# Cross-attention and mixture-of-experts kernel: unrolled two-expert tiles taken two at a time by TensorE

## The chip, the cores and the metric

One core of a Trainium2 chip runs the whole kernel in one launch. The metric is the device time of one execution in microseconds; the median of three runs is taken. The core's engines are TensorE (matrix products and transposes, results in PSUM), VectorE, ScalarE, GpSimd (named POOL in the profile, here mostly the issuer of gathers) and SyncE, which issues DMAs. Each works through its own list of instructions in order and waits on semaphores that the others raise.

## The reference

After a layer norm and a cross-attention, whose softmax is added to x, the second half is a mixture of experts over 1024 rows of 256 numbers. 64 experts have 64 hidden features each, and every row goes to 4 of them:

```python
_, topk_idx = jax.lax.top_k(logits + router_bias, K)          # K = 4
...
g = jnp.einsum('nd,edf->enf', flat, Wg)
u = jnp.einsum('nd,edf->enf', flat, Wu)
h = jax.nn.silu(g) * u
hw = h * combine.T[:, :, None]
out = jnp.einsum('enf,efd->nd', hw, Wd)
for i in range(Sg.shape[0]):                                   # 2 shared experts
    sh = jax.nn.silu(flat @ Sg[i]) * (flat @ Su[i])
    out = out + sh @ Sd[i]
```

The kernel computes only the chosen experts' products: rows are gathered into tiles by expert, and the results are gathered back and summed with their weights. All is float32.

## The kernel before

Attention, norms, routing and the lists of rows take the first 63 us. Then come tiles of 128 rows. The first `NP` = 32 tiles are unrolled, and each serves two experts: lanes 0 to 63 hold rows of expert 2q, lanes 64 to 127 rows of expert 2q+1. After them come tiles for the rows that did not fit, one expert each, whose experts are known only at run time; two turns of `U` = 4 such tiles are unrolled and the rest is a hardware loop. At the end the shared experts' products are computed and the results are gathered back.

One tile passes through these operations:

- GpSimd gathers 128 rows into `xg`, four buffers (L362; semaphore `got`). The gather of tile t waits for the transposes of tile t-4.
- TensorE transposes the two halves of the tile into bank `pb0` or `pb1` (L1014, semaphore `xT_ps`). It first waits for `xT_sb`, the copy of tile q-2 that empties the bank.
- VectorE copies the bank to `xgT`, two buffers (L805, semaphore `xT_sb`).
- TensorE makes the first product, gate and up together, into `pb2` or `pb3` (L1047, `gu_ps`). For a two-expert tile it is four matmuls of 64 output lanes each, half of the array's columns ("128*64" in the profile). One-expert tiles use two matmuls on the whole array (L1051).
- ScalarE applies silu to the gate half (L494, `silu_ok`).
- VectorE multiplies it with the up half into `hh2`, two instructions, one for each expert's lanes (L819, `h_ok`).
- TensorE transposes `hh2` into bank `pb7` (L1070, `hT_ps`); ScalarE copies it to `hT` (L503, `hT_sb`).
- TensorE makes the second product into `pb4` or `pb5` (L1083, `y_ps`), ScalarE copies it to `ysb` (L513, `y_sb`), and SyncE stores it.

The order is written out by hand. `over_tiles` calls each engine's function `step` for s = 0, 1, 2, ... and `which(lag)` gives it tile s - lag. In step s TensorE takes the input transposes of tile s, the first product of tile s-1, the `hh2` transpose of tile s-2 and the second product of tile s-3. VectorE takes the copy of tile s and `hh2` of tile s-1; ScalarE the silu of s-1, `hT` of s-2 and `ysb` of s-3.

VectorE carries other work in the same list, behind `hh2` of its step: one-hots for the token lists (`one_hot`, L680 and L682, s = 1, 3, 5, 7), a reduction (L835, s = 9), the token list (`tokens`, s = 11), the tiles' experts (`tile_experts`, L745 on, s = 12), two choices in each of s = 13 to 28 (`pick_choice`, L768) and the weights of the choices (`weights_of_choices`, L775 on, s = 29). ScalarE's `value` (L476) and TensorE's `list_tokens` (L984) belong to the token lists too.

Of the kernel before, what the change touches and what calls it, by code (L numbers as in the profile page):

```python
# [33 lines left out]
DC = D // P  # L34
HB = P // 2
NP = E // 2
MAXOV = 64
# [11 lines left out]
U = 4  # L49
# [10 lines left out]
def build_xattn_moe(nc, x, proj, amask, kmask, router, task, b2, rbias, shared, wgu, wd, out):  # L60
# [3 lines left out]
    with ExitStack() as ctx:  # L64
# [341 lines left out]
        def _(act):  # L406
# [75 lines left out]
            for n in range(1, EARLY):  # L482
                unit(n)

            def step(which, k, first, s):

                tile = which(1)
                if tile:
                    pair, q, m, r = tile
                    n = m % 2  # L490
                    act.wait_ge(gu_ps, q + 1 if pair else q + (NP + 1))
                    if not pair or q >= 2:
                        act.wait_ge(h_ok, q - 1 if pair else q + (NP - 1))
                    a.activation(sg[:, n, :], pb[2 + n][:, 0:F], ACT.Silu).then_inc(silu_ok, 1)  # L494
                tile = which(2)
                if tile:
                    pair, q, m, r = tile
                    n = m % 2
                    at = q if pair else q + NP
                    act.wait_ge(hT_ps, at + 1)  # L500
                    if not pair or q >= 2:
                        act.wait_ge(y_ps, at - 1)
                    a.activation(hT[:, n, :], pb[7][:, 0:P], ACT.Identity).then_inc(hT_sb, 1)  # L503
                tile = which(3)
                if tile:
                    pair, q, m, r = tile
                    n = m % YB
                    act.wait_ge(y_ps, q + 1 if pair else q + (NP + 1))
                    if pair and q >= YB:
                        act.wait_ge(y_out[n], 16 * (q // YB))  # L510
                    elif not pair:
                        act.wait_ge(y_out[n], r * (16 // YB) + 16 * NP // YB)
                    a.activation(ysb[:, n, :], pb[4 + m % 2][:, 0:D], ACT.Identity).then_inc(y_sb, 1)  # L513
                if s in (2, 4, 6, 8):
                    value((s - 2) // 2, MAXOV, NR)

            over_tiles(act, step, 4, lambda: (turn_count(act), last_turn_end(act)))
            for n in range(EARLY, len(units)):
# [365 lines left out]
        def _(pe):  # L884
# [115 lines left out]

            pe.wait_ge(unit_sb, 2)

            def step(which, k, first, s):

                tile = which(0)
                if tile:
                    pair, q, m, r = tile
                    n = m % 2
                    at = q if pair else q + NP
                    pe.wait_ge(got[m], 16 * (q // XB + 1) if pair else r * (16 // XB) + (NP // XB + 1) * 16)  # L1010
                    if not pair or q >= 2:
                        pe.wait_ge(xT_sb, at - 1)
                    for h in range(DC):
                        ins = t.transpose(pb[n][:, h * P:(h + 1) * P], xg[:, m, h::DC], ident[:, :])  # L1014
                    ins.then_inc(xT_ps, 1)

                if s == NP - 2:

                    pe.wait_ge(at_ok, 2)
                    for reg, e in zip(next_gu, load_at(0)):  # L1020
                        pe.reg_mov(reg, e)
                if s is None or s >= NP:

                    if k == 0:
                        gu_of[:] = [pe.snap(reg, min_val=0, max_val=E - 1) for reg in next_gu]
                    if k < D_LAG - GU_LAG:
                        if s is None or s >= NP + U:
                            d_of[k] = pe.snap(last_gu[k], min_val=0, max_val=E - 1) // 2
                    else:
                        d_of[k] = gu_of[k - (D_LAG - GU_LAG)] // 2  # L1030
                tile = which(GU_LAG)
                if tile:
                    pair, q, m, r = tile
                    n = m % 2
                    at = q if pair else q + NP
                    pe.wait_ge(xT_sb, at + 1)
                    if pair and q == 0:
                        pe.wait_ge(unit_sb, 2 * EARLY)
                    if not pair or q >= 2:
                        pe.wait_ge(h_ok, at - 1)  # L1040
                    if pair:
                        if q % 4 == 0:
                            pe.wait_ge(ld_gu[q // 4], 16)
                        for c in range(DC):
                            for g in range(2):
                                h = slice(g * HB, (g + 1) * HB)
                                ins = t.matmul(pb[2 + n][h, 0:2 * F], xgT[:, n, c, h], wgu_sb[:, 2 * q + g, c, :],  # L1047
                                               start=(c == 0), stop=(c == DC - 1))
                    else:
                        for h in range(DC):  # L1050
                            ins = t.matmul(pb[2 + n][:, 0:2 * F], xgT[:, n, h, :],  # L1051
                                           wgu_sb[:, bass.ds(gu_of[k], 1), h, :].rearrange("p o f -> p (o f)"),
                                           start=(h == 0), stop=(h == DC - 1))
                    ins.then_inc(gu_ps, 1)
                if (s is None or s >= NP) and k == U - 1:
                    for reg, e in zip(last_gu, gu_of[U - (D_LAG - GU_LAG):]):
                        pe.reg_mov(reg, e)
                if (s is None or s >= NP) and k == 1:
                    for reg, e in zip(next_gu, load_at(first + U)):
                        pe.reg_mov(reg, e)  # L1060
                tile = which(2)
                if tile:
                    pair, q, m, r = tile
                    n = m % 2
                    at = q if pair else q + NP
                    pe.wait_ge(h_ok, at + 1)
                    if not pair or q >= 1:
                        pe.wait_ge(hT_sb, at)
                    if pair:
                        t.transpose(pb[7][:, 0:P], hh2[:, n, :], ident[:, :]).then_inc(hT_ps, 1)  # L1070
                    else:
                        t.transpose(pb[7][:, 0:P], hh[:, n, :, :].rearrange("p a f -> p (a f)"), ident[:, :]).then_inc(hT_ps, 1)  # L1072
                tile = which(D_LAG)
                if tile:
                    pair, q, m, r = tile
                    n = m % 2
                    at = q if pair else q + NP
                    pe.wait_ge(hT_sb, at + 1)
                    if not pair or q >= 2:
                        pe.wait_ge(y_sb, at - 1)  # L1080
                    if pair and q % 8 == 0:
                        pe.wait_ge(ld_d[q // 8], 16)
                    t.matmul(pb[4 + n][:, 0:D], hT[:, n, :],  # L1083
                             wd_sb[:, q, :] if pair else wd_sb[:, bass.ds(d_of[k], 1), :].rearrange("p o d -> p (o d)"),
                             start=True, stop=True).then_inc(y_ps, 1)
                if s in (4, 6, 8, 10):
                    list_tokens((s - 4) // 2, MAXOV, NR, 192)
                if s == 10:
                    pe.wait_ge(cmp_ok, 2)
                    t.matmul(pb[6][:, 320:320 + MAXOV], ones_bf[0:E, :], cmp[:, :], start=True, stop=True,  # L1090
                             skip_group_check=True).then_inc(expert_ps, 1)

            gu_of, d_of = [None] * U, [None] * U

# [73 lines left out]
```

## Time and profile before

| | |
|---|---|
| median of 3 runs | 218.74 us (216.85 to 219.05) |
| profiled execution | 218.63 us, its span 216.9 us |
| TensorE busy | 175.2 us, 81% of the span |
| VectorE busy | 133.2 us, 61% |
| GpSimd busy | 111.2 us, 51% |
| ScalarE busy | 88.7 us, 41% |
| mean granted TensorE clock | 0.949 |

The span runs from the first to the last instruction; times in the rows are microseconds from its start. PE is TensorE's matmul side, PEld its weight loads, DVE is VectorE, ACT ScalarE. Consecutive instructions of one line are merged in a timeline row, with their count behind the x. A matmul's duration reaches to the arrival of its last result, and the next one starts earlier, so the pace of TensorE is read from start to start. A float32 product shows two records for each instruction, a transpose one. A bracket names the idle time of the engine ahead of the row and what ended it.

### The profile page before, as it was taken

To read this page: it belongs to the slowest core of one execution; us is meant where nothing else is said; L and a number is where in the kernel's file an instruction comes from. 1 tells how busy PE (TensorE), PEld (TensorE's weight loads), DVE (VectorE), ACT (ScalarE), POOL (GpSimd) and SP (SyncE) were. 2 spreads that over 40 slices of the span, in tenths; PEclk is the share of its full clock that TensorE was granted. 3 is DMA by queue.
4 is the path that set the end of the run, shared out by engine and by line. 5 is a ranking of instruction groups with operands and counts; after the bars stand their busy time and mean duration, and the time that the engine had idled before them with its cause. 6 is when DMAs were issued, how large, how long until landed. Compare 5 with 4: busy or idle time off the path is not lost.

```text
span 216.9 us, 4118 instructions
## 1 busy us (share of the span) xinstructions
PE 175.2 (81%) x964; PEld 124.1 (57%) x965; DVE 133.2 (61%) x528; ACT 88.7 (41%) x270; POOL 111.2 (51%) x121
## 2 busy tenths in 40 slices
PE   0980259999789999999999979999998979978300
PEld 0460148654435787777777968888863457437200
DVE  2995982175896574899997755556640450485450
ACT  2637378315522565565555654555552110120000
POOL 6692211001067454576666674676402777677740
PEclk9999999999855899999999999999999999999975
DMA  6899999995022333355454342544321333244432
GB/s 137 269 385 349 348 359 366 384 363 177 0 59 78 110 91 116 107 151 154 142 145 118 112 129 76 145 132 126 113 86 65 110 92 104 85 122 144 126 119 69
DMA packets 29825, 34.50 MB, mean 159 GB/s; under 512 B 4248, under 2 KB 27561, under 8 KB 29680
## 3 DMA queue, kind: packets, MB, share of 16 engines
q1 hardware_dynamic: 25392, 25.90, 36.1%
q0 software_dynamic: 4416, 8.41, 15.0%
q8 instruction: 7, 0.11, 0.3%
q14 instruction: 10, 0.08, 0.1%
HBM read 27.99 MB, written 9.96 MB: 175 GB/s over the span
## 4 chain that ended last, share of the span: by engine, by line
PE 68%; DVE 14%; ACT 4%; issue 4%; POOL 4%; DMA 3%; POOLq 1%; DVEq 0%; ACTq 0%
PE pb L1083 13%; PE pb L923 12%; PE pb L1047 9%; PE pb L1014 7%; PE pb L1051 6%; PE pb L1070 4%; PE pb L1119 3%; POOL z L394 3%; PE pb L984 2%; PE pb L1072 2%; DVE sc L558 2%; DMA proj_sb<-in_proj 2%; PE pb L888 2%; PE pb L894 2%; PE pb L908 2%
## 5 line engine op out<-in xcount | busy, mean ns | idle before, releaser
L362 POOL DMA_INDIRECT xg<-z_rows,tok x32 | 32.9, 1029 | 29.1 <-issue 11.6
L394 POOL DMA_INDIRECT z<-y_slots,slot_i x32 | 32.5, 1017 | 21.4 <-DMA y_slots<-ysb 11.3
L1083 PE MATMUL pb<-wd_sb,hT 128*128 128x256 f32 (+1 forms) x120 | 37.6, 396 | 0.0
L374 POOL DMA_INDIRECT xg<-z_rows,tok_now x28 | 27.9, 998 | 14.4 <-issue 11.5
L923 PE MATMUL pb<-zT,shared_sb 128*128 128x512 f32 x64 | 33.5, 675 | 0.7 <-ACT ysb L513 0.7
L805 DVE COPY xgT<-pb 128x256 f32<-128x256 f32 x60 | 25.3, 423 | 11.6 <-PE pb L1014 10.6
L513 ACT ACTIVATE ysb<-pb 128x256 f32<-128x256 f32 x60 | 23.0, 383 | 12.2 <-PE pb L1083 11.4
L1014 PEld LDWEIGHTS pb<-ident,xg 128*128 128x128 f32 x120 | 22.7, 198 | 8.4 <-issue 5.3
L1014 PE MATMUL pb<-ident,xg 128*128 128x128 f32 x120 | 25.5, 296 | 2.0 <-issue 1.4
L494 ACT ACTIVATE sg<-pb 128x64 f32<-128x64 f32 x60 | 13.4, 223 | 30.1 <-PE pb L1047 19.1
L1047 PE MATMUL pb<-wgu_sb,xgT 128*64 128x128 f32 x256 | 22.4, 299 | 0.3 <-DVE xgT L805 0.3
L859 DVE SCALAR_TENSOR_TENSOR xs<-z,wgt,xs 128x256 f32<-128x256 f32 x32 | 15.5, 483 | 10.4 <-DMA z<-y_slots,slot_i 8.5
L923 PEld LDWEIGHTS pb<-zT,shared_sb 128*128 128x128 f32 x64 | 13.0, 211 | 15.0 <-issue 14.8
L1083 PEld LDWEIGHTS pb<-wd_sb,hT 128*128 128x128 f32 x120 | 19.9, 206 | 1.7 <-issue 0.4
L824 DVE SCALAR_TENSOR_TENSOR hh<-sg,parity,pb 128x64 f32<-128x64 f32 x56 | 13.2, 278 | 9.5 <-ACT sg L494 9.0
L464 ACT ACTIVATE qkT<-pb 128x512 f32<-128x512 f32 x8 | 4.8, 597 | 32.7 <-PE pb L923 32.7
L1119 PE MATMUL pb<-shared_sb,hsh 128*128 128x256 f32 x64 | 14.6, 384 | 4.4 <-DVE hsh L789 2.8
L819 DVE TENSOR_TENSOR hh<-sg,pb 64x64 f32<-64x64 f32 x64 | 13.9, 217 | 6.1 <-ACT sg L494 4.4
L1051 PE MATMUL pb<-wgu_sb,xgT 128*128 x112 | 17.7, 280 | 0.0
L503 ACT ACTIVATE hT<-pb 128x128 f32<-128x128 f32 x60 | 16.5, 276 | 2.5 <-PE pb L1072 1.2
L1047 PEld LDWEIGHTS pb<-wgu_sb,xgT 128*64 128x64 f32 x256 | 14.2, 143 | 5.1 <-DVE xgT L805 1.2
L1119 PEld LDWEIGHTS pb<-shared_sb,hsh 128*128 128x128 f32 x64 | 11.9, 190 | 7.9 <-DVE hsh L789 4.5
(166 smaller groups left out, 242.9 us busy)
## 6 DMA issues: line engine op xcount, KB each, us to landing
wgu_sb<-in_wgu SPq DMA_DIRECT2D x8, 1024.0 KB, 10.4
y_slots<-ysb SPq DMA_DIRECT2D x60, 128.0 KB
wd_sb<-in_wd SPq DMA_DIRECT2D x4, 1024.0 KB, 11.6
shared_sb<-in_shared SPq DMA_DIRECT2D x1, 1536.0 KB, 9.3
xs<-in_x SPq DMA_DIRECT2D x4, 256.0 KB, 4.1
z_rows<-z SPq DMA_DIRECT2D x4, 256.0 KB, 9.1
out<-xs SPq DMA_DIRECT2D x8, 128.0 KB, 1.9
xg<-z_rows,tok POOLq DMA_INDIRECT x32, 2.9
```

The costliest lines, as they stand in the source:

```text
L362: g.indirect_dma_start(xg[:, n, :], None, z_dram, bass.IndirectOffsetOnAxis(ap=tok[:, t:t + 1], axis=0), bounds_check=N - 1, oob_is_err=Fa ...
L374: g.indirect_dma_start(xg[:, n, :], None, z_dram, bass.IndirectOffsetOnAxis(ap=tok_now[:, n:n + 1], axis=0), bounds_check=N - 1, oob_is_er ...
L394: g.indirect_dma_start(z[:, j % NC, :].bitcast(I32), None, y_dram, bass.IndirectOffsetOnAxis(ap=slot_i[:, 0, j:j + 1].bitcast(U32), axis=0 ...
L503: a.activation(hT[:, n, :], pb[7][:, 0:P], ACT.Identity).then_inc(hT_sb, 1)
L513: a.activation(ysb[:, n, :], pb[4 + m % 2][:, 0:D], ACT.Identity).then_inc(y_sb, 1)
L805: v.tensor_copy(xgT[:, n, :, :], pb[n][:, 0:D].rearrange("p (c n) -> p c n", c=DC)).then_inc(xT_sb, 1)
L923: ins = t.matmul(pb[2 * (n % 2) + g][:, :], sgu_sb[:, i, g, h, hc * P:(hc + 1) * P], zT[:, h, blk * 512:(blk + 1) * 512], start=(h == 0), ...
L1014: ins = t.transpose(pb[n][:, h * P:(h + 1) * P], xg[:, m, h::DC], ident[:, :])
L1047: ins = t.matmul(pb[2 + n][h, 0:2 * F], xgT[:, n, c, h], wgu_sb[:, 2 * q + g, c, :], start=(c == 0), stop=(c == DC - 1))
L1051: ins = t.matmul(pb[2 + n][:, 0:2 * F], xgT[:, n, h, :], wgu_sb[:, bass.ds(gu_of[k], 1), h, :].rearrange("p o f -> p (o f)"), start=(h == ...
L1083: t.matmul(pb[4 + n][:, 0:D], hT[:, n, :], wd_sb[:, q, :] if pair else wd_sb[:, bass.ds(d_of[k], 1), :].rearrange("p o d -> p (o d)"), sta ...
L1119: ins = t.matmul(pb[4 + i % 4][:, 0:D], hsh[:, q, i * P:(i + 1) * P], sd_sb[:, q, :], start=(q == 0), stop=(q == NSH * DC - 1))
```

## The change

Only TensorE's and ScalarE's lists change; GpSimd's, SyncE's and VectorE's stay as they are. For the unrolled two-expert tiles TensorE does nothing in even steps, and in an odd step s it takes two tiles through each operation: input transposes of s-1 and s, `hh2` transposes of s-5 and s-4, first products of s-3 and s-2, second products of s-5 and s-4. The two `hh2` transposes go side by side into bank `pb7`, and ScalarE copies both in one instruction. ScalarE's list follows: in odd steps that copy, two silus, two copies of `ysb`. In the last of these steps (s = 31) both engines take tile 30 or 28 once more through some operations, so that from s = 32 the old order holds. The core of the diff, for TensorE and then ScalarE (the operations themselves moved unchanged into functions of a tile):

```diff
+            def transpose_two_h(q):
+
+                pe.wait_ge(h_ok, q + 2)
+                if q:
+                    pe.wait_ge(hT_sb, q)
+                for n in range(2):
+                    ins = t.transpose(pb[7][:, n * P:(n + 1) * P], hh2[:, n, :], ident[:, :])
+                ins.then_inc(hT_ps, 2)
...
+            def two_tiles(s):
+
+                transpose_x(static_tile(s - 1))
+                transpose_x(static_tile(s))
+                if s >= 5:
+                    transpose_two_h(s - 5)
+                if s >= 3:
+                    first_product(static_tile(s - 3), None)
+                    first_product(static_tile(s - 2), None)
+                if s >= 5:
+                    second_product(static_tile(s - 5), None)
+                    second_product(static_tile(s - 4), None)
+
             def step(which, k, first, s):
 
+                if s is not None and s < NP:
+                    if s % 2 == 0:
+                        return
+                    two_tiles(s)
+                    if s in (5, 7, 9, 11):
+                        list_tokens((s - 5) // 2, MAXOV, NR, 192)
...
+                    if s == NP - 1:
+
+                        pe.wait_ge(at_ok, 2)
+                        for reg, e in zip(next_gu, load_at(0)):
+                            pe.reg_mov(reg, e)
+                        first_product(static_tile(NP - 2), None)
+                        transpose_two_h(NP - 4)
+                        second_product(static_tile(NP - 4), None)
+                    return
```

```diff
+            def copy_two_hT(q):
+
+                act.wait_ge(hT_ps, q + 2)
+                if q:
+                    act.wait_ge(y_ps, q)
+                a.activation(hT[:, :, :], pb[7][:, 0:2 * P].rearrange("p (n l) -> p n l", n=2), ACT.Identity).then_inc(hT_sb, 2)
...
             def step(which, k, first, s):
 
+                if s is not None and s < NP:
+                    if s % 2 == 0:
+                        return
+                    if s >= 5:
+                        copy_two_hT(s - 5)
+                    if s >= 3:
+                        silu(static_tile(s - 3))
+                        silu(static_tile(s - 2))
+                    if s >= 5:
+                        copy_y(static_tile(s - 5))
+                        copy_y(static_tile(s - 4))
```

TensorE's list of before in the middle of the unrolled tiles, two tiles long; the numbers are buffers and banks, `xg` into `pb0` or `pb1` is an input transpose, `wgu_sb` a first product, `hh2` its transpose, `wd_sb` a second product:

```order
131 L1014 MATMUL pb1<-ident,xg 128x128 [waits xT_sb,got3]
132 L1014 MATMUL pb1<-ident,xg 128x128
133 L1047 MATMUL pb2<-wgu_sb,xgT 64x128 [waits h_ok,xT_sb]
134 L1047 MATMUL pb2<-wgu_sb,xgT 64x128 x3
135 L1070 MATMUL pb7<-ident,hh2 128x128 [waits hT_sb,h_ok]
136 L1083 MATMUL pb4<-wd_sb,hT 128x256 [waits ld_d1,y_sb,hT_sb]
137 L1014 MATMUL pb0<-ident,xg 128x128 [waits xT_sb,got0]
138 L1014 MATMUL pb0<-ident,xg 128x128
139 L1047 MATMUL pb3<-wgu_sb,xgT 64x128 [waits h_ok,xT_sb]
140 L1047 MATMUL pb3<-wgu_sb,xgT 64x128 x3
141 L1070 MATMUL pb7<-ident,hh2 128x128 [waits hT_sb,h_ok]
142 L1083 MATMUL pb5<-wd_sb,hT 128x256 [waits y_sb,hT_sb]
```

The same work in the changed kernel, two tiles in one step:

```order
192 L1049 MATMUL pb0<-ident,xg 128x128 [waits xT_sb,got2]
193 L1049 MATMUL pb0<-ident,xg 128x128
194 L1049 MATMUL pb1<-ident,xg 128x128 [waits xT_sb,got3]
195 L1049 MATMUL pb1<-ident,xg 128x128
196 L1094 MATMUL pb7<-ident,hh2 128x128 [waits hT_sb,h_ok]
197 L1094 MATMUL pb7<-ident,hh2 128x128
198 L1067 MATMUL pb2<-wgu_sb,xgT 64x128 [waits ld_gu5,h_ok,xT_sb]
199 L1067 MATMUL pb2<-wgu_sb,xgT 64x128 x3
200 L1067 MATMUL pb3<-wgu_sb,xgT 64x128 [waits h_ok,xT_sb]
201 L1067 MATMUL pb3<-wgu_sb,xgT 64x128 x3
202 L1106 MATMUL pb4<-wd_sb,hT 128x256 [waits y_sb,hT_sb]
203 L1106 MATMUL pb5<-wd_sb,hT 128x256 [waits y_sb,hT_sb]
```

The second input transpose (row 194) now stands directly behind the first, ahead of the step's products. VectorE's list in the stretch with choices, as it stands in the changed kernel and, but for line numbers, in before; `xgT` is the copy, `hh2` the product with silu, `pick` a choice:

```order
203 L840 COPY xgT<-pb0 128x256 [waits gu_ps,xT_ps]
204 L854 TENSOR_TENSOR hh2<-sg,pb3 64x64 [waits hT_ps,silu_ok]
205 L854 TENSOR_TENSOR hh2<-sg,pb3 64x64
206 L803 SCALAR_TENSOR_TENSOR z,pick<-slotmap,slot8,logit 128x64 x2
207 L840 COPY xgT<-pb1 128x256 [waits gu_ps,xT_ps]
208 L854 TENSOR_TENSOR hh2<-sg,pb2 64x64 [waits hT_ps,silu_ok]
209 L854 TENSOR_TENSOR hh2<-sg,pb2 64x64
```

Nothing moves here: a copy of tile s, then `hh2` of tile s-1, tile by tile.

## Rows read from the trace of the kernel before

**Rows 1.** Page, chain of work that ended last: shares by engine

```profile
PE 68%; DVE 14%; ACT 4%; issue 4%; POOL 4%; DMA 3%; POOLq 1%; DVEq 0%; ACTq 0%
```

**Rows 2.** Stretches: length, busy PE PEld DVE ACT POOL, clock, DMA share, GB/s

```profile
51.50:58.30 6.80, 5.64 (x43) 3.43 (x42) 6.14 (x23) 5.11 (x11) 0.00 (x0) 1.00 0.04 14
58.30:72.00 13.70, 12.79 (x54) 6.66 (x54) 10.63 (x47) 3.42 (x10) 8.99 (x8) 0.50 0.23 62
...
86.30:119.60 33.30, 33.30 (x287) 25.79 (x287) 28.62 (x145) 18.96 (x65) 20.94 (x21) 1.00 0.48 135
```

**Rows 3.** Timeline (start, duration, operation), all engines, one two-expert tile

```profile
95.86 0.66 PE L1047 MATMUL pb<-wgu_sb,xgT 128*64 128x128 f32 x8
...
96.45 0.33 PE L1070 MATMUL pb<-ident,hh 128*128 128x128 f32 x1
...
96.56 0.22 ACT L494 ACTIVATE sg<-pb 128x64 f32<-128x64 f32 x1 [0.44 <-PE pb L1047]
...
96.81 0.28 ACT L503 ACTIVATE hT<-pb 128x128 f32<-128x128 f32 x1
96.82 0.45 DVE L819 TENSOR_TENSOR hh<-sg,pb 64x64 f32<-64x64 f32 x2
...
97.05 0.39 PE L1014 MATMUL pb<-ident,xg 128*128 128x128 f32 x2
...
97.30 0.29 DVE L768 SCALAR_TENSOR_TENSOR z<-slotmap,slot,logit 128x64 f32<-128x64 f32 x1
...
97.37 0.66 PE L1047 MATMUL pb<-wgu_sb,xgT 128*64 128x128 f32 x8
...
97.83 0.42 DVE L805 COPY xgT<-pb 128x256 f32<-128x256 f32 x1
```

**Rows 4.** Timeline, TensorE, one one-expert tile on the whole array

```profile
120.86 0.39 PE L1014 MATMUL pb<-ident,xg 128*128 128x128 f32 x2
121.09 0.61 PE L1051 MATMUL pb<-wgu_sb,xgT 128*128 x4
...
122.08 0.39 PE L1014 MATMUL pb<-ident,xg 128*128 128x128 f32 x2
```

**Rows 5.** Timeline, the first tiles, at half clock, with one-hots

```profile
67.37 1.12 PE L1047 MATMUL pb<-wgu_sb,xgT 128*64 128x128 f32 x8
67.60 0.43 DVE L680 TENSOR_TENSOR oh_tile<-lanes,slot_h 128x512 f16<-128x512 f16 x1
...
68.54 0.23 ACT L494 ACTIVATE sg<-pb 128x64 f32<-128x64 f32 x1 [1.46 <-PE pb L1047]
68.66 0.42 DVE L805 COPY xgT<-pb 128x256 f32<-128x256 f32 x1
...
69.00 0.44 DVE L819 TENSOR_TENSOR hh<-sg,pb 64x64 f32<-64x64 f32 x2
```

**Rows 6.** Timeline, the gather of tile 3, and the landings of the first gathers

```profile
64.52 1.67 POOL L362 DMA_INDIRECT xg<-z_rows,tok  x1 [0.30 <-PE pb L1014]
...
DMA to landing us min/median/max: 2.7/2.8/2.8
```

**Rows 7.** Timeline, VectorE: reduction, tile experts, weights of choices, and the copies behind

```profile
83.87 0.69 DVE L835 TENSOR_REDUCE zden<-logit 128x8 f32<-128x512 f32 x1
...
89.71 0.23 DVE L745 TENSOR_SCALAR tile_e<-pb 128x64 int32<-128x64 f32 x1
...
90.87 0.41 DVE L805 COPY xgT<-pb 128x256 f32<-128x256 f32 x1
...
115.38 0.19 DVE L775 TENSOR_REDUCE zden<-pick 128x8 f32<-128x32 f32 x1
...
116.27 0.42 DVE L805 COPY xgT<-pb 128x256 f32<-128x256 f32 x1
```

**Rows 8.** Timeline, TensorE: the first product of tile 28

```profile
113.94 0.66 PE L1047 MATMUL pb<-wgu_sb,xgT 128*64 128x128 f32 x8
```

**Rows 9.** Timeline, POOL: one gather behind another without a wait

```profile
122.81 1.00 POOL L374 DMA_INDIRECT xg<-z_rows,tok_now  x1 [0.30 <-issue]
```

More of the change, by code:

```diff
@@ L483, in _, with static_tile, silu @@
                 unit(n)
-            def step(which, k, first, s):
+            def static_tile(q):
+                return (True, q, q % U, q - q % U)
+            def silu(tile):
+                pair, q, m, r = tile
+                n = m % 2
+                act.wait_ge(gu_ps, q + 1 if pair else q + (NP + 1))
+                if not pair or q >= 2:
+                    act.wait_ge(h_ok, q - 1 if pair else q + (NP - 1))
+                a.activation(sg[:, n, :], pb[2 + n][:, 0:F], ACT.Silu).then_inc(silu_ok, 1)
@@ L487, in step @@
                 tile = which(1)
                 if tile:
[L489 to L494, printed above, removed]
+                    silu(tile)
                 tile = which(2)
                 if tile:
-                    pair, q, m, r = tile
@@ L498, in step @@
[L498 to L503, printed above, removed]
+                    copy_hT(tile)
                 tile = which(3)
                 if tile:
-                    pair, q, m, r = tile
-                    n = m % YB
-                    act.wait_ge(y_ps, q + 1 if pair else q + (NP + 1))
@@ L509, in step @@
[L509 to L515, printed above, removed]
+                    copy_y(tile)
             over_tiles(act, step, 4, lambda: (turn_count(act), last_turn_end(act)))
@@ L1001, in _, with static_tile, transpose_x @@
             pe.wait_ge(unit_sb, 2)
-            def step(which, k, first, s):
+            def static_tile(q):
+                return (True, q, q % U, q - q % U)
+            def transpose_x(tile):
+                pair, q, m, r = tile
+                n = m % 2
+                at = q if pair else q + NP
+                pe.wait_ge(got[m], 16 * (q // XB + 1) if pair else r * (16 // XB) + (NP // XB + 1) * 16)
+                if not pair or q >= 2:
+                    pe.wait_ge(xT_sb, at - 1)
+                for h in range(DC):
+                    ins = t.transpose(pb[n][:, h * P:(h + 1) * P], xg[:, m, h::DC], ident[:, :])
+                ins.then_inc(xT_ps, 1)
@@ new lines, in first_product @@
+            def first_product(tile, k):
+                pair, q, m, r = tile
+                n = m % 2
+                at = q if pair else q + NP
+                pe.wait_ge(xT_sb, at + 1)
+                if pair and q == 0:
+                    pe.wait_ge(unit_sb, 2 * EARLY)
+                if not pair or q >= 2:
+                    pe.wait_ge(h_ok, at - 1)
+                if pair:
+                    if q % 4 == 0:
+                        pe.wait_ge(ld_gu[q // 4], 16)
+                    for c in range(DC):
+                        for g in range(2):
+                            h = slice(g * HB, (g + 1) * HB)
+                            ins = t.matmul(pb[2 + n][h, 0:2 * F], xgT[:, n, c, h], wgu_sb[:, 2 * q + g, c, :],
+                                           start=(c == 0), stop=(c == DC - 1))
+                else:
+                    for h in range(DC):
+                        ins = t.matmul(pb[2 + n][:, 0:2 * F], xgT[:, n, h, :],
+                                       wgu_sb[:, bass.ds(gu_of[k], 1), h, :].rearrange("p o f -> p (o f)"),
+                                       start=(h == 0), stop=(h == DC - 1))
+                ins.then_inc(gu_ps, 1)
@@ new lines, in transpose_h @@
+            def transpose_h(tile):
+                pair, q, m, r = tile
+                n = m % 2
+                at = q if pair else q + NP
+                pe.wait_ge(h_ok, at + 1)
+                if not pair or q >= 1:
+                    pe.wait_ge(hT_sb, at)
+                if pair:
+                    t.transpose(pb[7][:, 0:P], hh2[:, n, :], ident[:, :]).then_inc(hT_ps, 1)
+                else:
+                    t.transpose(pb[7][:, 0:P], hh[:, n, :, :].rearrange("p a f -> p (a f)"), ident[:, :]).then_inc(hT_ps, 1)
@@ new lines, in transpose_two_h, with second_product @@
+            def transpose_two_h(q):
[5 more added lines that the diff above has]
+                ins.then_inc(hT_ps, 2)
+            def second_product(tile, k):
+                pair, q, m, r = tile
+                n = m % 2
+                at = q if pair else q + NP
+                pe.wait_ge(hT_sb, at + 1)
+                if not pair or q >= 2:
+                    pe.wait_ge(y_sb, at - 1)
+                if pair and q % 8 == 0:
+                    pe.wait_ge(ld_d[q // 8], 16)
+                t.matmul(pb[4 + n][:, 0:D], hT[:, n, :],
+                         wd_sb[:, q, :] if pair else wd_sb[:, bass.ds(d_of[k], 1), :].rearrange("p o d -> p (o d)"),
+                         start=True, stop=True).then_inc(y_ps, 1)
@@ L1005, in step @@
                 tile = which(0)
                 if tile:
[L1007 to L1030, printed above, removed]
+                    transpose_x(tile)
@@ L1031, in step @@
+                if k == 0:
+                    gu_of[:] = [pe.snap(reg, min_val=0, max_val=E - 1) for reg in next_gu]
+                if k < D_LAG - GU_LAG:
+                    if s is None or s >= NP + U:
+                        d_of[k] = pe.snap(last_gu[k], min_val=0, max_val=E - 1) // 2
+                else:
+                    d_of[k] = gu_of[k - (D_LAG - GU_LAG)] // 2
                 tile = which(GU_LAG)
                 if tile:
-                    pair, q, m, r = tile
-                    n = m % 2
@@ L1035, in step @@
[L1035 to L1053, printed above, removed]
@@ L1062, in step @@
                 if tile:
[L1063 to L1072, printed above, removed]
+                    transpose_h(tile)
                 tile = which(D_LAG)
                 if tile:
[L1075 to L1091, printed above, removed]
+                    second_product(tile, k)
             gu_of, d_of = [None] * U, [None] * U
```

34 lines of the change are left out of this document (31 added, 3 removed).

## The prediction

> **What bounds the kernel now.** The chain of waits comes first: TensorE holds 68% of it and VectorE 14% [rows 1]. The table by stretches then shows where. From 86.3 to 119.6 us, while the unrolled two-expert tiles run, TensorE is busy 33.30 of 33.30 us and VectorE 28.62 [rows 2]: TensorE sets the pace and VectorE has little room behind it. The timeline of one tile gives that pace: first product to first product is 97.37 - 95.86 = 1.51 us [rows 3]. The three engines lean on each other inside a tile: the product at 95.86 releases the silu on ScalarE at 96.56, that releases the product `hh2` on VectorE at 96.82, and behind this in VectorE's order stand two choices (`pick_choice`) and then the copy of the next transposed input at 97.83. All of it is hidden in before, because TensorE needs each of these results only about a tile later.
>
> **What the change takes away.** A tile changes TensorE's shape twice: `gu` uses half the columns (128*64), all else the whole array. A full-array tile later, with the same amount of arithmetic, takes 122.08 - 120.86 = 1.22 us [rows 4]. I put the whole difference, 1.51 - 1.22 = 0.29 us, down to the two changes. Two tiles now share them, so a pair needs 2 x 1.51 - 0.29 = 2.73 us of TensorE in place of 3.02. Over 15 pairs that is at most 4.4 us. ScalarE makes one copy of 128x256 where two of 128x128 took 0.28 us each [rows 3]. At most 0.28 us a pair is saved there, between 0 (one that costs as much as two) and that; ScalarE is not on the path in either case, since the copy (released by the transposes) is over before the silu behind it is released. I count 0.
>
> **What the change adds.** VectorE's order is untouched: copy(q), hh2(q-1), extra work, copy(q+1), and so on. TensorE's isn't. Call s = 2j+5 the step in which the inputs 2j+4 and 2j+5 are transposed. Input 2j+5 goes to the bank that copy(2j+3) must have emptied. Copy(2j+3) stands behind hh2(2j+1), that behind copy(2j+2), that behind hh2(2j). And hh2(2j) needs the first product of 2j, which TensorE now makes only in step 2j+3, one pair earlier, behind the transposes. TensorE waits at the head of its step for VectorE to go through two tiles' work that could only begin in the middle of the step before; queued behind the waiting transpose are both `hh2` transposes, both first and both second products. That is a closed ring. Its length from the first product of one pair to that of the next:
>
> - first product to silu 96.56 - 95.86 = 0.70, silu to hh2 96.82 - 96.56 = 0.26 [rows 3];
> - hh2 to what follows it on VectorE 97.30 - 96.82 = 0.48 [rows 3], copy to hh2 where nothing is waited for 69.00 - 68.66 = 0.34 [rows 5], hh2 again 0.48;
> - the copy, 0.42 [rows 3], and 0.04 until a waiting engine starts (a product group ends at 95.86 + 0.66 = 96.52, its silu starts at 96.56), 0.46;
> - on TensorE the two transposes of that input 0.23 [rows 4], plus about 0.05 for a weight load that nothing hides, the first hh2 transpose 0.11, then from the second to the first product 0.32 - 0.11 = 0.21 (input transposes to product 97.37 - 97.05 = 0.32 [rows 3], less one transpose): 0.60.
>
> Sum: 0.70 + 0.26 + 0.48 + 0.34 + 0.48 + 0.46 + 0.60 = 3.32 us, already over the 3.02 of before and the 2.73 of TensorE's own work. Every extra piece in VectorE's order between hh2(2j) and copy(2j+3) now adds in full. Before it cost nothing: its cover was TensorE's work, and this cover is gone. The extras, from the time the first of them starts to the copy behind it: two choices 97.83 - 97.30 = 0.53 [rows 3]; one-hots 68.66 - 67.60 = 1.06 [rows 5]; reduction 0.7, tile experts 90.87 - 89.71 = 1.16, weights of choices 116.27 - 115.38 = 0.89 [rows 7]; for the token list, two small operations, I estimate 0.4.
>
> The ring is gone through from tile 0 to tile 28, fourteen times. I add it up in absolute time. **Start:** the first product of tile 0 now stands behind the transposes of tiles 2 and 3. The gather of tile 3 starts at 64.52 and takes 0.67 longer than its like, which land in 2.8 [rows 6], so it lands near 68.0; with the transposes and the change of shape at half clock, twice 0.32, the product starts at 68.6. **Pairs 1 and 2** (one one-hot each) fall in the time at half clock, which in before ends at 72 us [rows 2] and which I let last to about 80, since TensorE is idle more at the start. There first product to silu takes 68.54 - 67.37 = 1.17 and not 0.70 [rows 5], and the transposes and the change about 0.5 more: 3.32 + 1.06 + 0.97 = 5.35. In the second pair TensorE's own work, twice 2.73, with the token-list matmuls, some 0.9, is longer: 6.3. **Pairs 3 and 4**: 3.32 + 1.06 = 4.38 each. **Pair 5** (reduction): 4.0. **Pair 6** (token list, experts): 3.32 + 0.4 + 1.16 = 4.9. **Pairs 7 to 14** (two choices for each tile): 3.32 + 2 x 0.53 = 4.38 each, 35.0. Together 68.6 + 5.35 + 6.3 + 8.8 + 4.0 + 4.9 + 35.0 = 133.0 us for the first product of tile 28, which stands at 113.94 in before [rows 8]: 19.0 late. **The end** of the stage: the product of tile 30 waits for its copy behind the weights of choices, 0.70 + 0.26 + 0.48 + 0.89 + 0.46 = 2.79 after that of 28; then two transposes, a second product, two input transposes and the product of 31, some 5.2 in all where three tiles took 4.5: 0.7 more. The dynamic tiles and all that follows keep their work and order. Gathers, stores and `y_sb` waits only get more room.
>
> In all 19.7 us. The profiled execution took 218.63 us (span 216.9), which agrees with the median of the runs, 218.74: 218.63 + 19.7 gives **238 us**.
>
> **Rivals.**
> 1. *TensorE's clock falls in the stage.* In the ring TensorE works 2.73 of 4.38 us, 62%. The records tell both ways: from 51.5 to 58.3 it was busy 5.64 of 6.80 us, with short f16 matmuls, and ran at half clock (1.2 of 2.4 GHz) after; I see no full-clock row with a share near 62%. Each pair spent at half clock costs 0.97 more. Half of the 12 pairs: 6 us, 244 us; all of them: 250. The Trainium skill (TensorE: Matmul & The Clock Gate, "A second HAM failure mode") says that short idle gaps between groups of matmuls can make the clock swing; no row here shows it for gaps like these. Chance 0.2.
> 2. *Faster: TensorE remains the bound.* The place is the transpose of the second input: if copy(2j+3) were done by the time TensorE comes to it, pairs would take 2.73, and the stage would win 4.4 us less some 1.5 for the late start: 216 us. POOL would allow it, a gather being 1.00 + 0.30 us, 2.6 a pair [rows 9]. It decides once the ring is under 3.02; the ring has 3.32 without any extra, and 13 of the 14 gaps carry one of 1 us or more. The Trainium skill (TensorEngine Tiling (Array Packing), "Key Properties") says that changing the tiling mode drains the engine, by which fewer changes make this faster; the 0.29 us a tile agree, but it is no rule on the wait. Chance 0.07.
> 3. *The ring exists but is shorter*, by parts that I count whole and that overlap: with 0.7 less a pair 228 us. Chance 0.07. Forecast: 0.66.
>
> **How the numbers follow.** The forecast's own range is 0.25 us a ring each way and the clock's rise at 72 or later: 233 to 242. To hold 8 in 10 the range takes in most of rival 1 and part of 3: 231 to 247. A measurement here tells about 1% from no change. Slower by over 1% are the forecast, rival 1 and nearly all of 3: 0.91; faster 0.06; same 0.03.
>
> **What would show it.** Waits of TensorE's input transpose (or its weight load) for the copy of xgT on VectorE, about 1.6 us for each pair with choices (4.38 - 2.73) and 0.6 without; first products of even tiles 4.4 us apart there; VectorE waiting for the silu once a pair; TensorE busy near 60 to 70% in the stage; the product of tile 0 near 68.6; the dynamic stage with its old length, shifted. It is wrong if pairs are 2.7 or 3.0 us apart, if TensorE waits at the hh2 transpose and not at the input, or if the granted clock shows half speed after 80 us (rival 1).

## The result and the profile after

The changed kernel takes 238.97 us (median of 4 runs, 238.06 to 239.62) against 217.80 (216.06 to 219.05) for the kernel before on the same chip: 1.0975 times as long, 95% interval 1.0879 to 1.1072. The profiled execution took 239.04 us, its span 237.3. Against the profiled execution of before that is 20.4 us more, by the medians 21.2, where 19.7 was forecast. Medians are of all executions, ratios and intervals of the fast ones alone.

The head of the page and its chain of waits:

```profile
span 237.3 us, 4074 instructions
PE 178.4 (75%) x963; PEld 125.2 (53%) x965; DVE 132.5 (56%) x528; ACT 86.2 (36%) x255; POOL 111.1 (47%) x121
PE 52%; DVE 21%; issue 9%; ACT 7%; DMA 4%; POOL 3%; POOLq 1%; DVEq 0%; ACTq 0%
```

All engines have about the work they had. The chain, which held 68% TensorE and 14% VectorE [rows 1], now has 52 and 21. The table by stretches (length, busy time of PE, PEld, DVE, ACT, POOL with counts, clock, DMA share, GB/s) answers to [rows 2]:

```profile
98.00:133.00 35.00, 24.95 (x199) 17.73 (x196) 21.01 (x112) 12.28 (x39) 15.14 (x16) 1.00 0.31 96
```

In the stretch with choices TensorE was busy all of the time before. It is now busy 24.95 of 35.00 us, 71%, and no other engine is nearer to full: VectorE has 60%. That is what a ring of waits looks like. Who waits for whom, from 60 to 140 us (engine, line waited for: us in total, times, longest):

```profile
DVE hh L854 <- ACT sg L494: 30.0, 16, 4.1
PE pb L1049 <- DVE xgT L840: 14.0, 21, 1.6
```

TensorE waits at its input transposes (L1049) for the copy (L840), and VectorE waits 16 times, once a pair, for the silu. One turn of the ring, all engines (start, duration, operation, as in [rows 3]):

```profile
105.20 0.42 DVE L840 COPY xgT<-pb 128x256 f32<-128x256 f32 x1
...
105.78 0.48 PE L1049 MATMUL pb<-ident,xg 128*128 128x128 f32 x2 [0.87 <-DVE xgT L840]
...
106.40 1.09 PE L1067 MATMUL pb<-wgu_sb,xgT 128*64 128x128 f32 x16
...
107.10 0.22 ACT L494 ACTIVATE sg<-pb 128x64 f32<-128x64 f32 x1 [0.17 <-PE pb L1067]
107.36 0.45 DVE L854 TENSOR_TENSOR hh<-sg,pb 64x64 f32<-64x64 f32 x2 [1.73 <-ACT sg L494]
...
107.84 0.29 DVE L803 SCALAR_TENSOR_TENSOR z<-slotmap,slot,logit 128x64 f32<-128x64 f32 x1
...
108.37 0.42 DVE L840 COPY xgT<-pb 128x256 f32<-128x256 f32 x1
...
108.72 0.44 DVE L854 TENSOR_TENSOR hh<-sg,pb 64x64 f32<-64x64 f32 x2
...
108.94 0.47 PE L1049 MATMUL pb<-ident,xg 128*128 128x128 f32 x2 [0.39 <-DVE xgT L840]
109.19 0.29 DVE L803 SCALAR_TENSOR_TENSOR z<-slotmap,slot,logit 128x64 f32<-128x64 f32 x1
...
109.72 0.42 DVE L840 COPY xgT<-pb 128x256 f32<-128x256 f32 x1
...
110.29 0.48 PE L1049 MATMUL pb<-ident,xg 128*128 128x128 f32 x2 [0.87 <-DVE xgT L840]
...
110.91 0.88 PE L1067 MATMUL pb<-wgu_sb,xgT 128*64 128x128 f32 x12
```

Read from the product at 106.40: silu 0.70 later, `hh2` 0.26, the choices 0.48, a copy 0.53, `hh2` 0.35, the choices 0.47, the copy that matters 0.53, the transposes 0.57, the next product 0.62. That closes at 4.51 us.

### The profile page after: what moved, and what is told of

It is laid out like the page before. It is cut to its first block, busy times and chain, and to the rows that moved or that the text cites. A ratio compares the mean times of both kernels' runs of the same rounds, so it can differ in the third digit from the quotient of the medians.

```text
span 237.3 us, 4074 instructions
## 1 busy us (share of the span) xinstructions
PE 178.4 (75%) x963; PEld 125.2 (53%) x965; DVE 132.5 (56%) x528; ACT 86.2 (36%) x255; POOL 111.1 (47%) x121
## 4 chain that ended last, share of the span: by engine, by line
PE 52%; DVE 21%; issue 9%; ACT 7%; DMA 4%; POOL 3%; POOLq 1%; DVEq 0%; ACTq 0%
PE pb L958 13%; PE pb L1106 8%; PE pb L1049 7%; PE pb L1071 6%; PE pb L1067 5%; DVE xgT L840 4%; PE pb L1196 3%; POOL z L394 3%; DVE z L803 3%; DVE hh L854 3%; PE pb L1086 2%; DVE sc L593 2%; DMA proj_sb<-in_proj 2%; PE pb L1094 2%; PE pb L943 1%
## 5 line engine op out<-in xcount | busy, mean ns | idle before, releaser
L1049 PE MATMUL pb<-ident,xg 128*128 128x128 f32 x120 | 27.6, 316 | 18.0 <-DVE xgT L840 14.0
L1049 PEld LDWEIGHTS pb<-ident,xg 128*128 128x128 f32 x120 | 20.6, 202 | 29.8 <-issue 25.1
L854 DVE TENSOR_TENSOR hh<-sg,pb 64x64 f32<-64x64 f32 x64 | 13.8, 216 | 30.8 <-ACT sg L494 30.0
L840 DVE COPY xgT<-pb 128x256 f32<-128x256 f32 x60 | 25.3, 422 | 8.4 <-PE pb L1049 7.3
L1067 PE MATMUL pb<-wgu_sb,xgT 128*64 128x128 f32 x256 | 19.5, 298 | 0.6 <-DVE xgT L840 0.6
L1067 PEld LDWEIGHTS pb<-wgu_sb,xgT 128*64 128x64 f32 x256 | 15.1, 147 | 4.0 <-issue 2.8
L510 ACT ACTIVATE hT<-pb 128x256 f32<-128x256 f32 x15 | 5.7, 383 | 26.9 <-PE pb L1094 23.8
## 6 DMA issues: line engine op xcount, KB each, us to landing
wd_sb<-in_wd SPq DMA_DIRECT2D x4, 1024.0 KB, 11.8
```

Source lines behind the costliest of these rows:

```text
L840: v.tensor_copy(xgT[:, n, :, :], pb[n][:, 0:D].rearrange("p (c n) -> p c n", c=DC)).then_inc(xT_sb, 1)
L854: ins = v.tensor_tensor(hh2[h, n, h], sg[h, n, :], pb[2 + n][h, F:2 * F], ALU.mult)
```

## The experiments

The experiments ran in two groups, each on a chip of its own, both like the first one. The kernel before took 216.35 us (7 runs) beside the changed kernel again, VectorE's list in pairs, the transpose moved back and the first pair early; it took 216.79 (11 runs) beside the extra work moved, the two copies and the order of its own. Each ratio is to the kernel before of its own group. An earlier group, on a chip where the kernel before is slower, stands at the end.

**The changed kernel again**, to have it beside the experiments on one chip.

> The changed kernel as it is, so that it stands beside the experiments on one chip: the earlier group of experiments ran on a chip where the kernel before took 234 us and not 218. If this chip is like the first, 238 to 240 us with pairs 4.51 us apart; if it is like the second, about as long as the kernel with two copies, 250 us.

238.52 us, ratio 1.099 (1.0908 to 1.1072), pairs 4.52 us apart. Its trace shows one thing that the first did not: once more a stretch at half clock. The table by stretches before it, in it and a pair later:

```profile
92.20:96.70 4.50, 2.77 (x22) 1.85 (x20) 3.04 (x17) 1.25 (x5) 2.60 (x3) 1.00 0.32 91
96.70:100.20 3.50, 3.50 (x21) 2.69 (x20) 2.28 (x14) 1.19 (x4) 1.00 (x1) 0.51 0.18 50
101.30:105.80 4.50, 3.24 (x27) 2.34 (x26) 2.63 (x14) 1.60 (x5) 2.68 (x3) 1.00 0.44 128
```

In the 4.50 us ahead TensorE was busy 2.77; then the clock was at 1.2 GHz for 3.50 us. The pair took 4.81 us (products at 96.51 and 101.32) in place of 4.52. Its product, its silu, and the transposes that close the turn:

```profile
96.51 1.81 PE L1067 MATMUL pb<-wgu_sb,xgT 128*64 128x128 f32 x16
...
97.51 0.23 ACT L494 ACTIVATE sg<-pb 128x64 f32<-128x64 f32 x1 [0.45 <-PE pb L1067]
...
100.69 0.48 PE L1049 MATMUL pb<-ident,xg 128*128 128x128 f32 x2 [0.17 <-DVE xgT L840]
```

The silu follows its product by 1.00 us and not by 0.70, and these 0.30 are the whole loss. The rest of the slow stretch fell on work whose end nobody in the ring waits for, and the transposes at 100.69 had the full clock again.

**VectorE's list in pairs too.** In an odd step VectorE now does copy(s-1), hh2(s-3), copy(s), hh2(s-2), and only then the extra work of both steps. TensorE and ScalarE as changed.

```diff
+                if s is not None and s < NP:
+                    if s % 2 == 0:
+                        return
+                    for t in (s - 1, s):
+                        copy_x(static_tile(t))
+                        if s >= 3:
+                            times_silu(static_tile(t - 2))
+                    extra(s - 1)
+                    extra(s)
```

> The kernel with VectorE's list in pairs again, to compare with the changed kernel on the same chip. On the second chip its pairs were 3.75 us apart, since TensorE's semaphores of the odd product and of both second products arrived together, 1.1 us late; on a chip without that delay the theory (ring through VectorE's list) gives 2.75 to 2.9 us a pair and 217 to 220 us in all. Rival (the late semaphores come from this order of instructions and not from the chip): again 3.7 us a pair, about 227 us.

219.70 us (219.24 to 220.21), ratio 1.0132 (1.0054 to 1.0209): 18.8 us of the loss are gone by VectorE's order alone, with not one instruction less of work. Pairs are 2.92 us apart. The timeline of one pair:

```profile
99.95 1.09 PE L1086 MATMUL pb<-wgu_sb,xgT 128*64 128x128 f32 x16
...
100.65 0.22 ACT L494 ACTIVATE sg<-pb 128x64 f32<-128x64 f32 x1 [0.17 <-PE pb L1086]
100.72 0.42 DVE L840 COPY xgT<-pb 128x256 f32<-128x256 f32 x1 [0.26 <-PE pb L1086]
...
101.06 0.44 DVE L854 TENSOR_TENSOR hh<-sg,pb 64x64 f32<-64x64 f32 x2
...
101.53 0.42 DVE L840 COPY xgT<-pb 128x256 f32<-128x256 f32 x1
...
101.94 0.64 PE L1068 MATMUL pb<-ident,xg 128*128 128x128 f32 x4
```

The choices are over before the product is, so the copy at 100.72 waits 0.26 us for the product and `hh2` at 101.06 for nothing. All four transposes run in one piece at 101.94. From 97 to 115 us TensorE is never idle:

```profile
97.00:115.00 18.00, 18.00 (x165) 14.72 (x166) 15.73 (x88) 9.78 (x31) 12.14 (x13) 1.00 0.48 144
```

**Only the extra work moved.** The order copy, hh2, copy, hh2 stays as in the changed kernel, but all extra work of two steps stands between copy(s) and hh2(s-1) of an odd s, where VectorE waits for the silu anyway.

```diff
+                if which(0):
+                    copy_x(which(0))
+                if s is not None and s < NP and s % 2:
+                    extra(s - 1)
+                    extra(s)
+                if which(1):
+                    times_silu(which(1))
```

> The kernel with VectorE's extra work moved out of the ring, on a chip like the first one. The ring without extras measured as 4.51 - 2 x 0.53 = 3.45 us: pairs with choices 3.45 us apart, 224 to 227 us in all. Rival (the extra work is not what lengthens the ring): 4.5 us and 238.5.

226.29 us (225.82 to 226.79), ratio 1.0431 (1.0378 to 1.0485); pairs 3.58 apart (products at 103.29 and 106.87), 0.93 less than 4.51 where the extras were priced at 2 x 0.53 = 1.06. TensorE still waits, by less:

```profile
105.67 0.42 DVE L840 COPY xgT<-pb 128x256 f32<-128x256 f32 x1
...
106.24 0.48 PE L1059 MATMUL pb<-ident,xg 128*128 128x128 f32 x2 [0.46 <-DVE xgT L840]
```

So about 12 us of the loss are extra work inside the ring: 11.8 less than the kernel with two copies below, of the same group, 12.2 less than the changed kernel of the other group. The ring without extras is over 3.02 by itself, as the first sum had it (3.32 there, 3.58 here).

**The waiting transpose moved back in TensorE's list**, behind the first products; VectorE as changed.

```diff
                 transpose_x(static_tile(s - 1))
-                transpose_x(static_tile(s))
...
                     first_product(static_tile(s - 2), None)
+                transpose_x(static_tile(s))
```

> The kernel with the second input transpose behind the two first products again, on the same chip as the changed kernel. Ring as worked out: 3.26 us for a pair with choices, 224 to 229 us. Rival (TensorE's semaphores are late in any order): 3.65 us a pair as on the second chip, about 230 us.

221.99 us (219.71 to 223.25), ratio 1.020 (1.0073 to 1.0326); pairs 3.18 apart. TensorE in one pair:

```profile
106.00 1.28 PE L1067 MATMUL pb<-wgu_sb,xgT 128*64 128x128 f32 x16
107.20 0.50 PE L1049 MATMUL pb<-ident,xg 128*128 128x128 f32 x2
...
108.55 0.47 PE L1049 MATMUL pb<-ident,xg 128*128 128x128 f32 x2
```

Between 95 and 115 us only one input transpose waits, 0.2 us. What is left of the wait for the copy is 0.20 us a pair, at the weight load of the odd tile's product. The two cures, one in either engine's list, take away 18.8 and 16.5 us, and they have only the ring in common.

**Two copies by ScalarE instead of one.**

```diff
-                a.activation(hT[:, :, :], pb[7][:, 0:2 * P].rearrange("p (n l) -> p n l", n=2), ACT.Identity).then_inc(hT_sb, 2)
+                for n in range(2):
+                    a.activation(hT[:, n, :], pb[7][:, n * P:(n + 1) * P], ACT.Identity).then_inc(hT_sb, 1)
```

> The changed kernel with two copies by ScalarE in place of one, on a chip like the first one, beside the changed kernel's 238.5 us of the group before. The copies end before the silu behind them is released: pairs stay 4.51 to 4.55 us apart, the whole within 1 us. Rival: up to 0.2 us a pair, 3 us slower.

238.12 us (237.47 to 238.64), ratio 1.0959 (1.0902 to 1.1015), pairs 4.51: the same as the changed kernel. The joint copy saves ScalarE some time and the kernel nothing.

**The first pair early.** VectorE in pairs, and the first products of tiles 0 and 1 ahead of the transposes of tiles 2 and 3, to take back the late start.

```diff
+                if s == 3:
+                    first_product(static_tile(0), None)
+                    first_product(static_tile(1), None)
                 transpose_x(static_tile(s - 1))
                 transpose_x(static_tile(s))
```

> VectorE's list in pairs and, in TensorE's step 3, the first products of tiles 0 and 1 ahead of the transposes of tiles 2 and 3, so that they need not wait for the gather of tile 3. Theory (the late start costs what the product of tile 0 is late, 2.6 us, and ScalarE and VectorE can use the time): 1.5 to 2.5 us less than with VectorE's list in pairs alone, 215 to 217.5 us, level with or under the kernel before. Rival (the gap only moves to the transposes behind, which wait for the same gather): within 0.5 us of it.

220.82 us (219.28 to 222.74), ratio 1.0135 (1.0034 to 1.0236): no gain over the first cure (VectorE's list in pairs). Tile 0's product starts at 65.52 and not at 68.67, but tile 4's at 76.58, where it had been at 75.84. TensorE in between:

```profile
69.40 0.51 PE L1068 MATMUL pb<-ident,xg 128*128 128x128 f32 x2 [0.89 <-DVE xgT L840]
70.70 0.51 PE L1068 MATMUL pb<-ident,xg 128*128 128x128 f32 x2 [0.80 <-DMA xg<-z_rows,tok]
```

The gap only moved: the next transposes wait for their copy and for their gather. A later pair (products at 103.10 and 107.34) takes 4.24 us besides, since its transposes wait 1.21 us for a gather; that is most of the 1.6 us by which this trace is longer than that of the first cure.

**All three engines in pairs, in an order of their own.** Tiles 0 to 11 in the old order; from there TensorE takes two transposes, two first products, two `hh2` transposes and the second products of the pair before, and VectorE both copies, both hh2, then the extras, so that every result has most of a pair's time to arrive.

```diff
                 transpose_x(static_tile(s - 1))
                 transpose_x(static_tile(s))
...
+                first_product(static_tile(s - 3), None)
+                first_product(static_tile(s - 2), None)
+                transpose_two_h(s - 5)
+                if s > PAIR + 2:
+                    second_product(static_tile(s - 7), None)
+                    second_product(static_tile(s - 6), None)
```

> A version meant to beat both. Up to tile 12 the order of the kernel before, one tile at a time, so no late start; from tile 13 two at a time. VectorE takes both copies, then both hh2, then the extra work. TensorE takes the hh2 transposes behind the first products and the second products of the pair before behind those (one step later), so it waits for nothing that VectorE begins in the same step. Theory: pairs at TensorE's own 2.74 us against 3.02, nine of them, 2.5 us, less some 0.5 at the change of order: 214 to 215 us beside 216.4, 0.5 to 1.2% faster. Rival (VectorE, with 2.7 us of work a pair in the stretch with choices, becomes the bound): pairs at 2.9 to 3.0, no gain.

220.23 us (218.13 to 221.34), ratio 1.0128 (1.0070 to 1.0187), where a gain was expected; a miss. TensorE at the change of order, in a steady pair, and at the end:

```profile
89.81 0.47 PE L1074 MATMUL pb<-ident,xg 128*128 128x128 f32 x2 [1.41 <-DVE xgT L841]
90.21 1.09 PE L1092 MATMUL pb<-wgu_sb,xgT 128*64 128x128 f32 x16
...
93.68 0.51 PE L1074 MATMUL pb<-ident,xg 128*128 128x128 f32 x2 [1.65 <-DMA xg<-z_rows,tok]
94.12 1.09 PE L1092 MATMUL pb<-wgu_sb,xgT 128*64 128x128 f32 x16
...
96.85 1.09 PE L1092 MATMUL pb<-wgu_sb,xgT 128*64 128x128 f32 x16
97.88 0.44 PE L1119 MATMUL pb<-ident,hh 128*128 128x128 f32 x2
98.15 1.03 PE L1131 MATMUL pb<-wd_sb,hT 128*128 128x256 f32 x4
99.01 0.63 PE L1074 MATMUL pb<-ident,xg 128*128 128x128 f32 x4
99.58 1.09 PE L1092 MATMUL pb<-wgu_sb,xgT 128*64 128x128 f32 x16
...
116.61 1.13 PE L1131 MATMUL pb<-wd_sb,hT 128*128 128x256 f32 x4 [0.75 <-ACT hT L511]
```

The steady pair is 99.58 - 96.85 = 2.73 us, to the hundredth what the prediction worked out as TensorE's own need. Six of the seven gaps from 94.12 to 113.53 are within 0.12 of it. Three other places lose more. From the product of tile 11 to that of tile 12 (86.64 to 90.21) it takes 3.57 us, against 1.50 before: TensorE waits 1.41 us for a copy. The pair behind took 3.91 us, since TensorE has to wait for a gather: POOL issues one each 1.30 us there and had no lead. And from the product of tile 28 at 113.53 to the first dynamic product at 121.48 it takes 7.95 us, against 5.93 before: second products wait 0.75 and 0.52 us for their `hT`, and two more of them are left to do. Against before the three places lose 2.1, 0.9 and 2.0 us, while the seven pairs win 7 x 3.02 - (113.53 - 94.12) = 1.7. The loss is no greater than 1.6 us at the first dynamic product because this execution came to tile 11 already 1.6 us earlier than the profiled one of before (86.64 and 88.27), 1.0 of it at tile 0, which the new order does not touch.

**On another chip** four of these edits had been run before; the changed kernel itself was not. The kernel before takes 234.05 us (232.35 to 236.59) there. VectorE in pairs took 238.66 us, a ratio of 1.0230 (1.0150 to 1.0311), only the extras moved 243.21, 1.0386 (1.0292 to 1.0480), the transpose moved back 236.56, 1.0135 (1.0017 to 1.0254), two copies by ScalarE, which leaves the ring as it is, 250.38, 1.0727 (1.0645 to 1.0808). Two of the four expectations, as recorded there:

> TensorE's list stays as in the changed kernel; only VectorE's list follows it: in an odd step copy(s-1), hh2(s-3), copy(s), hh2(s-2), and then the extra work of both steps. Theory (ring through VectorE's old order): copy(2j+5) now needs only the first product of 2j+3 in the same step and no result that is a step away, so TensorE should hardly wait at the second input transpose; pairs in the stretch with choices come down from 4.51 us to 2.75 to 2.9, the whole to 217 to 220 us (the late start of about 2.5 us stays). Rival (TensorE's own order or its clock costs the time, not VectorE's): pairs stay over 4 us and the whole near 239.

> The changed kernel with two copies of 128x128 by ScalarE in place of the one for both transposed activations, each raising hT_sb by one. Theory: the copy is over before the silu behind it is released, so the one copy gains nothing and two cost nothing: within 0.5 us of the changed kernel. Rival: the silu of the first tile of the pair starts later by up to 0.2 us a pair, 15 pairs, 3 us slower.

The other two had 223 to 227 us for the extras moved and 224 to 229 for the transpose moved back. All three cures missed their times, which had been worked out from the first chip. Against the kernel with two copies they still take away 11.7, 7.2 and 13.8 us, so the ring costs time there too; the two best change places, within their intervals. The pairs are longer: with VectorE in pairs, most are about 3.75 us apart there and 2.92 on the first chip. The same piece of the timeline on that chip:

```profile
102.76 1.09 PE L1086 MATMUL pb<-wgu_sb,xgT 128*64 128x128 f32 x16
...
105.12 0.22 ACT L494 ACTIVATE sg<-pb 128x64 f32<-128x64 f32 x1 [1.33 <-PE pb L1086]
105.19 0.42 DVE L840 COPY xgT<-pb 128x256 f32<-128x256 f32 x1 [0.77 <-PE pb L1086]
105.24 0.65 ACT L520 ACTIVATE ysb<-pb 128x256 f32<-128x256 f32 x2
```

The second silu follows the start of the two product groups by 2.36 us, where VectorE in pairs had 1.14 above (99.95 to 101.09). So times of this chip are compared with no others.

## Why the prediction was right, and where it was off

**The mechanism.** Three edits that share only the ring, two in VectorE's list and one in TensorE's, take back about 12, 18.8 and 16.5 us of about 22. That TensorE waits at the head of its step for VectorE's list, and that this costs the time, is shown, not argued. The signs came as forecast: pairs near 4.4 apart, VectorE waiting for the silu once a pair, TensorE at 71% (60 to 70 was said), and the dynamic stage with its length (40.4 us from its first to its last first product, 40.2 before).

**The sum.** The first products of even tiles stand at 68.27, 73.64, 79.19, 83.71, 88.22, 92.39, 97.38 and then every 4.51 us up to 133.48, for tile 28. Term by term:

| term | predicted | measured |
|---|---|---|
| product of tile 0 | 68.6 | 68.27 |
| pair 1 | 5.35 | 5.37 |
| pair 2 | 6.3 | 5.55 |
| pairs 3 and 4 | 8.76 | 9.03 |
| pair 5 | 4.0 | 4.17 |
| pair 6 | 4.9 | 4.99 |
| pairs 7 to 14 | 35.0 | 36.10 |
| product of tile 28 | 133.0 | 133.48 |
| from 28 to 31 | 5.2 | 5.21 |

Two terms are off by more than a few tenths, with opposite signs, and the start is 0.3 us early; that the sum up to tile 28 is within 0.5 us owes something to luck. **The release of the transpose**: I took 0.04 us from the copy's end to TensorE's start, from a product group and its silu. The copy at 105.20 ends at 105.62 and the transposes start at 105.78, 0.16 later. That is 0.12 a turn, about 1.6 us in the thirteen turns that the ring bounds. The 0.05 for a weight load that nothing hides had no row behind it; here the transposes that waited take 0.31 us to what follows them (105.78 to 106.09), and 0.23 in [rows 4], so it is 0.08. With small roundings the two make 4.51 of 4.38. **Pair 2**: I let TensorE's half clock last to 80 us and held it to be the bound there, 6.3. TensorE in that pair:

```profile
72.62 0.67 PE L1049 MATMUL pb<-ident,xg 128*128 128x128 f32 x2
73.08 0.63 PE L1094 MATMUL pb<-ident,hh 128*128 128x128 f32 x2
73.64 1.98 PE L1067 MATMUL pb<-wgu_sb,xgT 128*64 128x128 f32 x16
...
77.42 1.17 PE L1019 MATMUL pb<-oh_val,sc 128*128 128x64 f16 x8
78.41 0.64 PE L1049 MATMUL pb<-ident,xg 128*128 128x128 f32 x4
...
79.19 1.09 PE L1067 MATMUL pb<-wgu_sb,xgT 128*64 128x128 f32 x16
```

It was indeed the bound: it runs on without a wait. But the clock rose at 78.3 us, just ahead of the transposes. At half clock two input transposes had taken 0.46 us (72.62 to 73.08) and the `hh2` transposes 0.56; four and two of them would be 1.48, and at 78.41 they took 79.19 - 78.41 = 0.78. These 0.70 us are nearly all of the 0.75 by which the term is off.

**What was not said.** TensorE waits at the first input transpose of a step as well, 0.39 us at 108.94: the copy two tiles back is late too. It adds nothing, since the second one waits for a later copy of the same list. The two waits make 0.39 + 0.87 = 1.26 us a pair, less than the 1.6 that was forecast for one: TensorE was busy for more than 2.73 us a pair, 3.24 of 4.50 in the stretch from 101.30. Two transposes that start after a wait show 0.48 us and not 0.39. And 2.73 was never reached in this order of operations, see rival 2.

**Rival 1, the clock.** After 78.3 us the changed kernel had the full clock through the stage in its first trace, and in its second one stretch of 3.50 us at 1.2 GHz, which cost 0.3 us. So the event that the rival needs does occur in this stage, rarely. The Trainium skill (TensorE: Matmul & The Clock Gate, "A second HAM failure mode") lets the clock swing with short idle gaps between groups of matmuls; one trace of the two agrees, by one swing, and does not show what set it off. The price of 0.97 a pair was about right for a pair that runs at half clock as a whole. Pair 1 does: it takes 5.37 us, and pair 3, with the same one-hot at the full clock, 83.71 - 79.19 = 4.52, so 0.85 less. The swing was cheap because it met only one of the ring's two pieces on TensorE.

**Rival 2, no ring.** Its 2.73 us for TensorE's own pair is right for one order, that of the kernel with an order of its own. With VectorE's list in pairs, in the changed kernel's order for TensorE, a pair takes 2.92 us though TensorE is never idle, so that pairing wins 0.10 us there and not 0.29. What the 0.19 between them are is not shown. VectorE's list may still hold TensorE by a little: the last `hh2` of the pair ends at 101.99 + 0.45 = 102.44, and its transposes start at 102.50. The Trainium skill (TensorEngine Tiling (Array Packing), "Key Properties") has the engine drained by a change of mode. The 0.29 us agree with that, but both orders change the mode twice a pair, so no run here gives the change a price of its own.

Its price of 216 us was too good. With the ring gone the kernels take 219.7 to 220.8, a ratio of 1.013 to 1.014, slower than before. Two tiles at a time need a gather more ahead. In the first cure the product of tile 4 comes at 75.84, in before at 74.47, and one later pair (90.30 to 94.11) takes 3.81 us since its transposes wait 0.79 us for a gather; its other pairs are too little shorter to win that back. The traces show 1.0 us of the difference (spans 217.9 and 216.9); the medians say about 3. The profiled execution of before, 218.63, is one of its longer ones: beside the experiments those with a mean granted clock of 0.948 to 0.950 take 217.84 to 218.76 us, as this one with 0.949, and the others, with 0.958 to 0.964, 215.90 to 217.34. How much of the 3 us this explains stays open, since the executions of the first cure have no such split.

No version here beats the kernel before: the intervals of all ratios above lie over 1.

## What to carry to other kernels

Before taking the stages of two tiles together on an engine that works in order, write down the list of every engine that answers it, and follow a result from where it is made to where it comes back. What was one tile of slack becomes a closed ring, and every piece of other work that stands in the answering list between the two can add its full time once a turn (here 0.93 of 1.06 us). Move such work to where that engine waits anyway, or give it the same pairs; and weigh what pairing saves (here 0.10 to 0.29 us a pair, by the order) against filling and emptying the longer pipe before you build it.

## What the runs showed of the hardware

From the end of a VectorE copy to the start of a transpose that waited for it, TensorE took 0.16 us here, while ScalarE starts 0.04 us after a product group ends [rows 3]. Each has to be read for its own pair of engines.

The ring took 5.37 us a turn at 1.2 GHz (pair 1) and 4.52 at 2.4 GHz with the same extra work (pair 3). A stretch of 3.50 us at 1.2 GHz, which ended before the transposes that close the turn, cost 0.3 us.

On the other chip the engines behind TensorE started late. By the trace the two product groups that start at 102.76 end at 102.76 + 1.09 = 103.85, and the silu of the second starts at 105.12, 1.27 us later; the `ysb` copies start right behind it, at 105.24. The same code has 0.05 us at this place on the chip of the experiments above (101.04 to 101.09). Why, stays open: nothing run here tells a late signal from a late end that the records don't show.
